# Mixture-of-experts stage of a small transformer stack: where the queue asks for the first W_down blocks, and where TensorE waits for the up weights

## The reference

```
logits = xf @ router_w.T                      # 4096 rows, 8 experts
top_w, top_i = lax.top_k(softmax(logits), 2)  # two experts per row
g = einsum('nd,ehd->neh', xf, w_gate)         # hidden size 512
u = einsum('nd,ehd->neh', xf, w_up)
h = silu(g) * u
y = einsum('neh,edh->ned', h, w_down)
out = einsum('ned,ne->nd', y, combine)        # only the two chosen experts count
```

## Time and profile before

| | us |
|---|---|
| median of three runs | 2429.17 |
| lowest and highest | 2426.43, 2437.65 |
| the profiled execution's own time | 2426.62 |
| its span, first to last instruction | 2424.8 |
| TensorE busy over the span | 2255.0 (93%) |
| VectorE, ScalarE, GpSimd busy | 1867.3 (77%), 1418.4 (58%), 881.3 (36%) |
| mean granted TensorE clock | 0.976 |

### The profile page before, as it was taken

How to read it: one execution, slowest core, us unless ns; L and a number is a source line. 1 busy time by engine, 2 the same in 40 slices (tenths; PEclk the granted TensorE clock), 3 DMA queues, 4 the chain that set the end, 5 groups by cost and what they waited for, 6 DMA issues and landing times. The chain is left out here.

```text
span 2424.8 us, 103467 instructions
## 1 busy us (share of the span) xinstructions
PE 2255.0 (93%) x44156; PEld 1859.8 (77%) x44156; DVE 1867.3 (77%) x3749; ACT 1418.4 (58%) x3825; POOL 881.3 (36%) x769
## 2 busy tenths in 40 slices
PE   7999999999998983999997899999999899999997
PEld 6888888888884553888886677777777678888886
DVE  5777777778885786666665788888889688888876
ACT  5656666656654553555554677777777255555555
POOL 3233333333322121444443733444423544343330
PEclk9999999999998995999998999999999999999999
DMA  6455555555432327455554688878777522222220
GB/s 206 139 160 151 155 160 149 158 155 156 112 81 61 103 74 303 157 162 158 160 160 162 191 237 235 228 222 235 218 220 219 166 77 77 78 83 81 74 79 29
DMA packets 230872, 365.56 MB, mean 151 GB/s; under 512 B 35208, under 2 KB 113676, under 8 KB 229136
## 3 DMA queue, kind: packets, MB, share of 16 engines
q1 hardware_dynamic: 223600, 342.16, 46.5%
q0 software_dynamic: 6816, 16.79, 2.0%
HBM read 203.75 MB, written 78.77 MB: 117 GB/s over the span
## 5 line engine op out<-in xcount | busy, mean ns | idle before, releaser
L878 ACT ACTIVATE prob_x<-ps_score_x,neg_max_x 128x257 f32<-128x257 f32 x1024 | 402.6, 479 | 201.2 <-DVE neg_max_x L950 201.2
L950 DVE TENSOR_REDUCE neg_max_x<-ps_score_x 128x2 f32<-128x514 f32 x512 | 328.8, 683 | 103.5 <-PE ps_score_x L757 102.5
L768 PEld LDWEIGHTS ps_v_x<-v_wide_x,probT_x 128*32 128x32 f32 x18432 | 288.4, 109 | 123.0 <-issue 107.8
L768 PE MATMUL ps_v_x<-v_wide_x,probT_x 128*32 128x68 f32 x18432 | 335.1, 224 | 20.2 <-DMA v_wide_x<-v_out_x 9.0
L974 DVE STREAM_TRANSPOSE probT_x<-prob_x 128x1152 f32<-128x1152 f32 x256 | 344.0, 1344 | 0.0
L1114 POOL TENSOR_TENSOR ctxT_x_lo<-ready,ctxT_x_hi 128x514 fp32r<-128x514 f32 x128 | 152.9, 1195 | 368.6 <-ACT ctxT_x_hi L857 305.5
L1114 POOL TENSOR_TENSOR split<-loaded,split 128x514 fp32r<-128x514 f32 x128 | 153.4, 1199 | 326.3 <-ACT split L857 326.1
L2644 POOL TENSOR_TENSOR cells_s<-cells_s,moved_s 128x512 f32<-128x512 f32 x128 | 172.7, 1361 | 260.1 <-DMA moved_s<-w_s 203.2
L1230 ACT ACTIVATE loaded<-loaded,neg_max_s 128x32 f32<-128x32 f32 x512 | 156.6, 308 | 121.1 <-DVE neg_max_s L1219 121.1
L249 PE MATMUL ps_x<-split,w_q_x_hi 128*128 128x258 f32 x1024 | 207.5, 299 | 15.7 <-POOL split L1114 11.9
L869 ACT ACTIVATE kT_x<-ps_x,bias_k 128x257 f32<-128x257 f32 x256 | 122.1, 478 | 127.0 <-PE ps_x L249 126.5
(11 more groups left out here) (317 smaller groups left out, 6030.1 us busy)
## 6 DMA issues: line engine op xcount, KB each, us to landing
v_wide_x<-v_x SPq DMA_DIRECT2D x512, 76.5 KB, 2.2
v_out_x<-v_x SPq DMA_DIRECT2D x128, 306.0 KB, 4.2
v_wide_x<-v_out_x SPq DMA_DIRECT2D x512, 76.5 KB, 3.1
w_raw_moe<-moe_down SPq DMA_DIRECT2D x71, 512.0 KB, 3.6
ready<-ctx SPq DMA_DIRECT2D x128, 257.0 KB, 3.4
loaded<-ctx SPq DMA_DIRECT2D x128, 257.0 KB, 4.0
moved_s<-w_s SPq DMA_DIRECT2D x256, 128.0 KB
gate_whole<-moe_experts SPq DMA_DIRECT2D x32, 256.0 KB
```

Source lines behind the costliest of these rows:

```text
L768: ins = pe.do.matmul(self.ps_v[r * T:(r + 1) * T, b % 2, :, :], self.probT[b % 3][:, r, n * T:(n + 1) * T], self.v_wide[b % 4][:, :, r, n, ...
L878: act.do.activation(self.prob[b % 3][:, r, 0:S], self.ps[:, r, 0:S], ACT.Exp, bias=self.neg_max[b % 2][:, r:r + 1]).then_inc(*s.exp.at(tag ...
L950: dve.do.tensor_reduce(self.neg_max[b % 2][:, r], self.ps[:, r, 0:S], AX_X, ALU.max, negate=True).then_inc(*s.neg_max.at(tag, b, half))
```

## The change

Two statements. SyncE, which has read tile 0's row number into its register, waits for the first two gathers of rows to land before it asks for W_down's first block; all later blocks stand behind that. TensorE makes `turn_x(0)` ahead of its wait for the up weights instead of behind it.

```
         for t in range(N_TILES):
             row = self.nc.values_load(self.w_row[0:1, t:t + 1], ...)
+            if t == 0:
+                for ahead in range(2):
+                    sp.wait_ge(s.x_fetched[ahead], ahead)
             if t >= 4:
                 sp.wait_ge(s.down_lo, "w", t - 4)
             sp.do.dma_start(self.w_raw[t % 4], self.w_down[bass.ds(row, P), :]).then_inc(*s.w_fetched[t % 4].at(t))
...
         code()
         pe.wait_ge(s.plan, "hi_at")
+        turn_x(0)
         pe.wait_ge(s.e_in, "up_hi")
-        turn_x(0)
         for t in range(N_TILES + 1):
```

## The result

| | before | after |
|---|---|---|
| median of 20 runs, us | 2431.53 | 2426.16 |
| lowest and highest | 2424.19, 2437.78 | 2420.33, 2431.20 |
| ratio, with its 95% interval | | 0.998 (0.997 to 0.9989) |
| span of the profiled execution | 2424.8 | 2429.4 |

A ratio of 0.998 is 4.9 us less, with an interval of 2.7 to 7.3 us; the two medians lie 5.4 us apart. Forecast were 3.65 us less and 2425.5 us. The interval leaves out 1, so the change is faster, if only by 0.2%. The span of the one profiled execution after is longer than that of before: single executions of either kernel lie up to 14 us apart, so the two spans say nothing of the change.

A forecast was written before the change was run, and what follows sets the result against it. TensorE was taken as the bound, idle at the experts' start until the first gather landed. Gather -3.65, first block 0, order of waits 0, clock 0: 2429.17 - 3.65 = 2425.5 us, range 2420.5 to 2431.5.

The forecast's parts named there:

- The bound: Experts' stage: TensorE fully busy in the steady part, so time won at the beginning passes to the end one for one.
- The gather: Start of the experts' stage: without W_down's traffic the first gather lands 3.65 us earlier (bounds 2.2 to 4.3).
- The added wait: SyncE's queue: W_down's first block asked for 6.65 us later, still 2.1 us ahead of use; cost taken as 0.
- The order of TensorE's waits: First transposes ahead of the wait for up weights, which landed before the gather anyway; value 0.
- The clock: First tile on TensorE: full clock again about 3.1 us behind the first gate matmul, moving with it; effect 0.
- (a): First gather slow by itself, from a first use of GpSimd's queue; time as before, 2429.2 us; chance 0.20.
- turns between the queues: DMA engines alternate between queues by packet, so the first gather gains at most some 0.4 us; about 2428.8 us.
- (b): Gather 2, outside the wait, is overrun by W_down's blocks; TensorE waits up to 0.7 us, 2426.3 us; chance 0.12.
- (c): W_down's first block lands too late for ScalarE, gain lost; with 8.5 us to landing 2430.3 us; chance 0.05.

The follow-up runs named there:

- turn_only: Kernel before with only tile 0's transposes moved ahead of TensorE's wait for the up weights; ratio to before 0.9993 (0.998 to 1.0005).
- wait_only: Kernel before with only SyncE's wait for the first two gathers ahead of W_down's first block; ratio to before 0.9982 (0.997 to 0.9995).
- late_block: Changed kernel with W_down's first block asked for only after TensorE's transposes of tile 1; ratio to before 0.9994 (0.9979 to 1.0009).

## Why the prediction was right

**The bound.** Idle time of TensorE at the stage's beginning went over to the end of the stage: down(0) 3.2 us sooner, the last tile 2.2 us sooner from the first gather's issue (356.9 against 359.1), with the short tiles of the execution before, 1.0 us, between the two. `turn_only` and `wait_only`, whose tiles took 340.2 and 339.9 us, have the last tile at 360.3 and 356.5: 3.8 us apart. Beyond the stage no trace could show it; the 20 runs of each kernel do, with 4.9 us (2.7 to 7.3), and 3.65 lies inside. But so do 3.2 and 4.0: the time bears out that the gain goes through to the end, and not the forecast's last half microsecond.

**The gather.** Expected at 3.55 us after its issue, measured at 3.2. With the median of the later gathers alone, 3.3, it would have been hit: the 0.25 us that I added for GpSimd's longer first instruction weren't there. Its gain is 4.0 us, not 3.65.

**The added wait.** The second gather took 2.8 us, not 3.3, SyncE issued at 4.61 us after the first gather's issue (957.00; forecast 5.03), and the block landed 2.8 us ahead of its use (960.6 against 963.37), where 2.1 were forecast. Cost 0, as taken. `late_block` bears out the slack behind it.

**The order of TensorE's waits.** Value 0, as taken, by `turn_only` and `wait_only`.

**The clock.** This is the term that was mis-sized: taken as 0, measured +0.8 us. The full clock came 3.14 us behind the first gate matmul before (961.79 to 964.93) and 4.86 us behind it after (957.53 to 962.39); 1.7 us more at 0.45 us each make 0.8. Nothing shows it to be a cost of the change: over the kernels without fillers the full clock came 3.1 to 6.1 us behind the first gate matmul, in no order by the number of blocks ahead, and before was at the low end. Taking before's 3.1 as fixed was the mistake; one trace couldn't tell. The other error, that of the gather, was less than half as large and went the other way, and the sum came out 0.45 us too large for the first tile.

**The rivals.** (a) is out, by the change's own trace and by the kernels with three blocks ahead. With it goes the use that I made of turns between the queues: by it three blocks ahead should have cost some tenths of a microsecond; they cost 2.4 to 3.4. I had taken turns of equal bytes; were a turn a whole block, it would last 512 KB at the 346 GB/s of rows 1, 1.5 us (an estimate), and that is still less than was lost. The rule stands in the Trainium skill ("DMA: Bandwidth & Descriptors", section "Queues, rings and completion order": engines take turns between queues, packet by packet). The trace agrees with it for the last 2.3 us before the landing, in which the packets of both queues move side by side, and shows nothing of it for the 4.6 us before, in which only SyncE's do; there the measurement decides. What keeps the gather from starting, the fetching of its descriptors (the orders to the engines, one for each piece of data) or something in the memory, no run here shows. (b) did not come: gather 2 landed 5.7 us after the first gather's issue in the change, ahead of all W_down blocks. But gather 3, issued 0.4 us ahead of the first block, took 4.4 us (2.8 in `late_block`, where no block was asked for until 6.3 us after it), and in a stage that needed it at once it would have been late. So blocks asked for just behind a gather slow it too. (c) did not come either, and its price is now known.

## What to carry to other kernels

- When a small transfer starts a stage and large ones can wait, let the large ones' queue wait for the small one's landing; even one block ahead cost the gather 0.6 us here. Work out from the trace where the large one's data is first used: here it was asked for 6.2 us later (4.6 us behind the first gather's issue instead of 1.6 ahead of it) and still came 2.8 us early, with 1.3 us of slack behind that.
- Where TensorE's first work after an idle stretch lies on the path, the half clock costs too: 2.2 to 2.5 us here, against the 4.0 of the gather. Some matmuls of constants in the idle time took that away from the traces (44 of them, ending 2.0 us before the data came); a gain in the program's time isn't shown.
- A gain of 0.2% in a kernel that scatters by 0.5% is found in the trace by counting from the last event that the edit doesn't touch, not in the spans.

## What the runs showed of the hardware that I had not expected

- A gather of 128 KB on GpSimd's queue took 3.1 to 3.4 us with nothing ahead, 3.8 with one block of 512 KB of SyncE's queue ahead, 3.7 and 4.1 with two, 5.6 and 6.6 with three, 6.7 and 7.2 with four (the third issued 0.04 us and the fourth 0.9 us after the gather), and 4.1 with four quarter blocks.
- What grows is above all the time until the first packet of GpSimd's queue moves: 2.0 us with none or one block ahead, 2.3 and 2.4 with two, 3.7 and 4.0 with three, 4.5 and 4.9 with four. Once it moves, the two queues' packets move side by side.
- The full clock (2.4 GHz) came 3.1 to 6.1 us behind the first gate matmul over the eleven profiled executions without fillers, with the same matmuls ahead of it and behind it and 5.4 to 9.3 us of idle time ahead of the transposes: 4.86 in the change, 3.5 and 6.1 in two executions of one kernel. At 0.45 us for each microsecond at half clock (1.2 GHz) that alone scatters the stage by 1.3 us. With the fillers the engine kept the full clock through idle times of 2.12 and 1.12 us.
